# Gated slot attention on one core: VectorE's gates between the running sums and their reciprocal, the turn of the inverse sums behind the score masks

## What is computed

```python
z = cumlogsumexp(s, axis=time)
g = exp(concat([z[:1], z[:-1]]) - z);  p = exp(s - z)
hk = hk * g_t[None, :] + k_t[:, None] * p_t[None, :]       # step over time
ok = einsum('k,km->m', q_t, hk)
pv = softmax(ok)
hv = hv * g_t[:, None] + p_t[:, None] * v_t[None, :]       # step over time
ov = einsum('m,mv->v', pv, hv)
out = (rmsnorm(ov) * g_norm_weight * gate * sigmoid(gate)) @ Wo
```

## Time and profile before

| what | value |
|---|---|
| median of 3 runs | 1366.8 us (1366.7 to 1366.85) |
| profiled execution, its time | 1366.91 us |
| profiled execution, its span | 1365.2 us |
| PE (TensorE matmul) busy | 1332.2 us, 98% |
| DVE (VectorE) busy | 1087.6 us, 80% |
| ACT (ScalarE) busy | 410.3 us, 30% |
| POOL (GpSimd) busy | 142.1 us, 10% |
| DMA engines, mean busy share on the SyncE queue | 44.8% |

### The profile page before, as it was taken

The page is one execution under the profiler, slowest core; times in us unless marked ns, Lnnn a source line. Parts: engine busy times, 40 slices in busy tenths (PEclk is TensorE's granted clock), DMA queues, the critical chain, the costliest instruction groups (busy, mean ns, idle before and its releaser), DMA issues.

```text
span 1365.2 us, 23090 instructions
## 1 busy us (share of the span) xinstructions
PE 1332.2 (98%) x8711; PEld 1112.2 (81%) x8711; DVE 1087.6 (80%) x1708; ACT 410.3 (30%) x1187; POOL 142.1 (10%) x106
## 2 busy tenths in 40 slices
PE   6999999999999999999999999999999999999998
PEld 5788888888888888888888888888888778888886
DVE  8888888888998899889988998899777865545354
ACT  4333323322332233223322332333223333222221
POOL 3001101110120021001100110111100010000000
PEclk9999999999999999999999999999999999999999
DMA  6147556655655565557555755575322530000000
GB/s 185 48 104 171 119 114 144 139 116 109 154 125 116 117 166 124 120 114 171 130 118 117 169 125 117 120 168 118 76 79 43 162 107 1 31 1 31 0 32 31
DMA packets 500554, 144.49 MB, mean 106 GB/s; under 512 B 359648, under 2 KB 491616, under 8 KB 500448
## 3 DMA queue, kind: packets, MB, share of 16 engines
q1 hardware_dynamic: 500448, 143.08, 44.8%
HBM read 85.80 MB, written 57.21 MB: 105 GB/s over the span
## 4 chain that ended last, share of the span: by engine, by line
PE 74%; DVE 22%; issue 2%; ACT 1%; DMA 1%; SPq 0%; POOL 0%; DVEq 0%
PE bank L487 14%; PE bank L489 13%; PE bank L488 13%; PE bank L118 13%; PE bank L1633 6%; DVE cT L1076 4%; PE bank L711 4%; DVE y L1189 2%; PE bank L619 2%; DVE cT L1073 2%; PE bank L632 2%; DVE oT_lo L1052 1%; PE bank L637 1%; PE bank L694 1%; DVE o L1157 1%
## 5 line engine op out<-in xcount | busy, mean ns | idle before, releaser
L487 PE MATMUL bank<-wvg_hi,xT_hi 128*128 128x512 f32 x512 | 205.7, 402 | 12.5 <-DVE g L1084 12.5
L489 PE MATMUL bank<-wvg_hi,xT_lo 128*128 128x512 f32 x512 | 199.8, 390 | 0.0
L488 PE MATMUL bank<-wvg_lo,xT_hi 128*128 128x512 f32 x512 | 199.6, 390 | 0.0
L771 ACT ACTIVATE a_and_v<-bank 128x256 f32<-128x256 f32 x128 | 49.0, 383 | 328.2 <-PE bank L489 328.2
L487 PEld LDWEIGHTS bank<-wvg_hi,xT_hi 128*128 128x128 f32 x512 | 96.2, 188 | 35.5 <-issue 16.1
L489 PEld LDWEIGHTS bank<-wvg_hi,xT_lo 128*128 128x128 f32 x512 | 96.1, 188 | 20.5
L488 PEld LDWEIGHTS bank<-wvg_lo,xT_hi 128*128 128x128 f32 x512 | 96.3, 188 | 17.9
L1076 DVE RECIPROCAL cT<-cT 128x512 f32<-128x512 f32 x32 | 107.3, 3353 | 1.1
L1024 POOL TENSOR_TENSOR rstd<-ssq,neg_half 128x8 f32<-128x8 f32 x32 | 52.4, 1636 | 509.3 <-DVE ssq L1131 509.3
L487 PE MATMUL bank<-wo_hi,oT_hi 128*128 128x512 f32 x256 | 99.9, 390 | 0.0
L489 PE MATMUL bank<-wo_hi,oT_lo 128*128 128x512 f32 x256 | 99.6, 389 | 0.0
(11 more groups left out here) (165 smaller groups left out, 3030.4 us busy)
## 6 DMA issues: line engine op xcount, KB each, us to landing
o_transposed<-o SPq DMA_DIRECT2D x27, 512.0 KB, 3.4
oT_lo<-o_transposed SPq DMA_DIRECT2D x108, 128.0 KB, 3.0
fp_weights<-q SPq DMA_DIRECT2D x28, 318.0 KB, 2.8
e_tokens<-k_tok_then_wT SPq DMA_DIRECT2D x31, 256.0 KB, 2.3
e_tok<-e_tokens SPq DMA_DIRECT2D x124, 64.0 KB, 2.4
c_tokens<-cT SPq DMA_DIRECT2D x31, 256.0 KB, 3.0
cT<-c_tokens SPq DMA_DIRECT2D x124, 64.0 KB, 2.3
w_slots<-p SPq DMA_DIRECT2D x27, 256.0 KB, 2.4
```

Of the source, the lines that this page charges most:

```text
L487: pe.matmul(dst, w_hi, m_hi, start=(k == 0), stop=False)
L488: pe.matmul(dst, w_hi, m_lo, start=False, stop=False)
L489: last = pe.matmul(dst, w_lo, m_hi, start=False, stop=(k == n - 1))
L771: return act.activation(dst, src, ACT.Copy)
```

## The change

`sums` is cut in three. It keeps the running sums. The reciprocal becomes `invert` and is called after gate 0 and before gate 1, so gate 0 stands between sums and reciprocal. The turn becomes `c_turn` and is called behind `mask_scores`. In the first prologue `invert(0)` follows `sums(0, 0)` directly, as before, and there was no turn there.

```diff
@@ sums, new functions
             dve.tensor_tensor_scan(c_sum, eT[i % 2][:, :], eT[i % 2][:, :], 0.0, ALU.add,
                                    ALU.bypass).then_inc(s_scan, 1)
+
+        def invert(u):
+
             dve.wait_ge(s_scan, u + 1)
             dve.reciprocal(c_sum, c_sum).then_inc(s_cinv, 1)
-            if u:
-                dve.wait_ge(s_cinv, u + 1)
-                dve.transpose(c_sum, c_sum).then_inc(s_cb, 1)
+
+        def c_turn(nu):
+
+            dve.wait_ge(s_cinv, nu + 1)
+            dve.transpose(c_sum, c_sum).then_inc(s_cb, 1)
@@ unit
                 k_turn(nu)
                 sums(nu, ni)
                 gate(0, nu, ni)
+                invert(nu)
                 gate(1, nu, ni)
             mask_value_weights(u, i)
@@ unit
             if not tail:
                 quantise(u, slice(2, 4))
             mask_scores(nu, ni)
+            c_turn(nu)
             if tail:
                 norm_tokens(i - 1, (0, 1))
             gate(2, nu, ni)
@@ prologue
         sums(0, 0)
+        invert(0)
```

## The result

| | before | with the change |
|---|---|---|
| median of 20 runs, us | 1366.84 (1366.05 to 1368.03) | 1364.99 (1361.26 to 1368.39) |
| ratio | | 0.9985, 95% interval 0.9979 to 0.9991 |
| profiled execution: time, span | 1366.91, 1365.2 | 1363.08, 1361.3 |

The kernel is 0.15% faster: 1.9 us where 5.9 were forecast. Its executions lie 7.1 us apart, those of before 2.0. The profiled one is the fifth fastest of the 20, 1.9 us under the median, so its waits are likely smaller than those of a typical execution.

A forecast was written before the change was run, and what follows sets the result against it. TensorE, busy 98% of the span, bounds the kernel. 12.5 us gained less 0.3, 3.6, 2.1 and 0.3 is 6.2; from 1366.9 that is 1360.7, plus 0.3 for GpSimd's splits: 1361.0 us, range 1355 to 1369.

The forecast's parts named there:

- What goes: TensorE's job VG2 (L487) waiting for VectorE's gate 0: all 17 waits end, 12.5 us gained.
- The keys of the next unit: `load_k` behind the later `store_c`, wanted by L619: a draw in index 1, only unit 1 waits, 0.3 us lost.
- The softmax weights: `load_w` behind `store_e`, wanted by L694 in index 2: units 2, 10 and 22 wait 1.1 to 1.3, 3.6 us lost.
- The estimate by the fit of the Trainium skill: 256 KB of Wk ahead of `store_e`: 0.6 us by about 2 us plus bytes at 436 GB/s; 0.15 less loss in three units.
- The first feed-forward weights: `load_gate_up(0)` behind unit 30's later `store_c`: `w_up` takes 6.7 us, L118 starts 0.65 later, 2.1 us lost.
- Unit 29's norm and GpSimd's splits: TensorE's transposes wait 0.3 us for unit 29's norm; later Ws and Wk splits meeting VectorE work add 0.3 us.
- The microsecond that I said this rule might give back: GpSimd's L985 slips under reciprocal and masks, turn up to 1.0 us earlier in every pair; sum 2 to 3 us better.
- The third rival: Units of index 2: a pair loses 0.4 to 0.9 us beyond before in nearly all seven; 1364 to 1369; chance 0.2.
- The slower one: L694 in seven units of index 2 loses 2.3 us a pair, 16 us: 1377; decides from 0.85 a pair; chance 0.12.

The follow-up runs named there:

- run 9: The changed kernel once more, unaltered, for a second profile: 1366.01 us, ratio 0.9988 against the kernel before.
- Run 8: Against the changed kernel, Wk is loaded ahead of the fp8 loads in units of index 2, turn still late: 1361.36 us.
- run 2: Against the changed kernel, gate 0 goes back behind the reciprocal, the turn stays late behind the score masks: 1375.75 us, ratio 1.0063 against the kernel before.
- run 10: Against the changed kernel, the turn stands later still, behind gate 2 and the first product with the gate: 1386.92 us, ratio 1.0149 against the kernel before.
- run 3: Against the changed kernel, the turn stands directly behind the reciprocal in the seven units of index 1 only: 1359.32 us.
- run 1: Against the changed kernel, the turn stands directly behind the reciprocal, ahead of gate 1, in all units: 1353.63 us, ratio 0.9898 against the kernel before.
- run 5: Against the changed kernel, the turn stands in the middle, between the value masks and the rounding steps: 1354.69 us.

## Why the prediction was wrong in size

**What goes**: right. All 17 waits ended; 13.4 us instead of 12.5, as each restart of TensorE behind a wait had cost another 0.05.

**In sum.** Of the 4.0 us between forecast (5.9) and result (1.9) the books of the profiled execution hold 1.8: 0.9 more gained, 2.0 more lost at L694, 1.5 by the clock, 0.2 at L619, and 0.3 each not lost in unit 1, in unit 29 and by GpSimd's splits, 0.1 less in the last unit. The rest lies between this execution and the median.

**The keys of the next unit** (point 1: a draw, 0.3 lost in unit 1): near in the first profile, where unit 1 lost nothing and unit 22 0.2, and too low in others. A draw between two times of which one scatters isn't 0 in the mean; it was 1.4 us in run 9.

**The softmax weights** (point 2: three units wait, 3.6 us): this step failed, in two of its terms. Place, mechanism and releaser were right, but five units wait, 5.3 us by the list of waits and 5.6 by the books. First, I took half of the upper bound for `store_e` behind Wk, 0.65 us over 2.3, and the first profile has 1.1 to 1.3, the whole of it; from `store_e` to `load_w` it is 5.4 to 5.8 us where I had 5.1. Run 8 shows that Wk in front of the store makes it. Second, I let the last piece of `load_w` go out 1.6 us after the first everywhere; in unit 10 it took a whole microsecond more, and its wait was 2.40 instead of 1.1 to 1.3. That is the larger part of the 1.7 by which the sum was short; units 18 and 26, which I had at "0.1 at most", make 0.87. Two things hid in this. That unit 22 came out at 1.04 against 1.05 is luck: the queue was 0.5 us less late than I had counted, and the store cost half a microsecond more. And the three pairs with the least time to spare were misread: from the end of Wk's issue to `store_e` unit 26 had 2.5 us, less than the 2.7 of unit 22. The estimate by the fit of the Trainium skill ("SBUF — State Buffer", section "The DMA setup-cost knee") was 0.6; the measured 1.1 to 1.3 decides.

**The clock**: missing altogether, put at nothing without a reason. A wait of 2.40 us in unit 10 cost 1.5 more, at a granted clock of 0.54, and those of 2.91 (run 2) and 2.19 us (run 10) in the same unit cost some 1.6 more, at 0.58 and 0.68. The four waits at L118 of 3.89 us and more (runs 8, 3, 9 and 10) were followed by stretches at 0.50 to 0.66, but six waits of 2.06 to 2.78 us by 1.00. So of the nine waits for a transfer between 2 and 3 us that the profiles hold three were followed by the slow clock, and all four of the longer ones. This, too, makes the late turns steep.

**The first feed-forward weights** (point 3: 2.1 lost): 2.0 in the first profile; in run 9 the wait was 1.6 longer, and the slow clock came on top. I took 6.7 us for `w_up` from one row of one execution; over the twelve profiles of this study it took 6.5 to 8.6.

**Unit 29's norm and GpSimd's splits** (0.3 each): unit 29 gained its full 1.50, and the books have no loss for the splits. The turn ended some 0.5 us earlier than I had counted, and not by what I weighed. In unit 21 gate 0, reciprocal and gate 1 took 3.92 us together where I had added up 4.22, because each starts a little ahead of the end of the one before. L985 did start earlier, at 750.00 in unit 21, but fell into the rounding steps again. VectorE's rows there:

```profile
749.81 0.81 DVE L1228 TENSOR_TENSOR q<-q,q8t 128x636 f32<-128x636 f32 x1
750.65 1.80 DVE L1229 TENSOR_TENSOR q<-q,q8t 128x636 f32<-128x636 f32 x1
```

And GpSimd's:

```profile
750.00 1.77 POOL L985 TENSOR_TENSOR wo_lo<-stage,wo_hi 128x512 fp32r<-128x512 f32 x1 [6.24 <-ACT wo_hi L771]
```

First GpSimd is held up by L1228 (1.77 instead of 1.29), then L1229 by GpSimd (1.80 instead of 0.82). That is as the Trainium skill has it ("SBUF — State Buffer", section "SBUF: two separate sides"): whoever starts first keeps the port to the end. The microsecond that I said this rule might give back did not come in this unit.

**The third rival** ("a pair loses 0.4 to 0.9 ... in nearly all seven units: 1364 to 1369") named the time that came, but not quite the way to it: five units waited, for 0.37 to 2.40 us, and part of the loss is the clock's and the last unit's. **The slower one** was right about its mechanism and far too mild: it put the deciding point at 0.85 us a pair at L694 alone. Runs 2 and 10 crossed over with `store_c` 0.7 to 1.4 and 0.9 to 1.5 us later in the units of index 1 (in run 10 still more in others), as L619 joined in, in up to 23 units.

**The root**: I summed differences of medians. Each of these terms is the larger of 0 and (landing minus need), with the need 0 to 1 us away, and landings that differ between executions, `w_up`'s by 2.1 us. Where a term sits at its edge, an early landing gives nothing and a late one costs in full, so its mean lies above its value at the median. It fits this that the executions lie 7 us apart in a kernel whose predecessor varied by 2, and that in runs 1 and 5, which take the terms off their edge, they lie 0.7 and 1.0 apart (four executions each). That the means work out so is argued, not measured by itself.

## What to carry to other kernels

When a step is moved that a transfer waits for, don't ask only whether that transfer is in time: take its queue in issue order and find the first place behind it where the queue used to be idle. What stands ahead of that place comes late by the whole delay (here `load_k`: in run 10 L619 waits for it in 23 units), what stands behind it by the delay less the spare time. Move the half of a change that relieves the bounding engine, and leave the half that feeds a shared in-order queue where it is: here the first half alone gives 1.0%, both together 0.15%, and the second alone costs 0.6%. And read the spread of the executions as a result: when it grows from 2 to 7 us, something that used to be hidden now ends in the critical path.

## What was unexpected of the hardware

A 256 KB store issued 0.48 us behind a 256 KB load on the same queue landed in 3.4 to 3.6 us in the first profile and in 3.3 to 3.9 in the other profile of the same kernel (run 9), against 2.3 alone and 2.5 behind three loads of 106 KB each. The first group of feed-forward weights (`w_up`, 768 KB, behind as much again) landed in 6.5 to 8.6 us over the twelve profiles, in 6.9 and 8.6 in the two of the changed kernel. After TensorE had waited for a transfer for 2.19, 2.40, 2.91, 3.89, 4.10, 4.21 and 5.85 us its granted clock was 0.50 to 0.68 in the next 3 to 4.4 us, that is, partly or wholly at the lower level; after 2.06, 2.08, 2.54, 2.56 and twice 2.78 us it was 1.00, so between 2 and 3 us the length of the wait alone doesn't tell which it will be. A GpSimd operation was itself lengthened by the VectorE operation that it met (1.77 instead of 1.29 us), and lengthened the next (1.80 instead of 0.82).
